# A graph network in four layers: the row fetches of its first two passes are made once a tile, and SyncE copies the rows to their places

## The chip, the cores and the metric

The kernel runs on one core of a Trainium2 chip. The metric is the device time of one execution in microseconds (us), the median of several runs.

## What is computed

The input is a graph of 5000 nodes with 128 features and 85,000 edges sorted by their destination. Four layers each take a layer norm and a ReLU of the node features, gather the rows of the source nodes, combine them over the edges of each destination node, and add the result to the features:

```python
edge_index = jnp.stack([src, dst])
h = jnp.maximum(_layernorm(x, axis=-1), 0.0)
x = x + _L0_gnn_ref(h, src, dst, L0_gnn_W, L0_gnn_b)            # mean of h[src] per dst, then a linear layer
h = jnp.maximum(_layernorm(x, axis=-1), 0.0)
x = x + _L1_gnn_ref(h, src, dst, L1_gnn_W_edge, ...)            # mean of relu(A h[src] + B h[dst]) per dst, then a linear layer
h = jnp.maximum(_layernorm(x, axis=-1), 0.0)
x = x + _L2_gnn_ref(h, edge_index, L2_gnn_W1, ...)              # two graph attention convolutions of 16 heads
h = jnp.maximum(_layernorm(x, axis=-1), 0.0)
x = x + _L3_gnn_ref(h, edge_index, L3_gnn_Wq, ...)              # dot-product attention of 2 heads over the edges
```

## The kernel before

The edges lie in 665 tiles of 128 (`T`), one edge on each partition, and the nodes in 40 blocks of 128 (`NB`). A step is one pair of a tile and a block that has destinations in it. Since the edges are sorted, a tile at the border of two blocks makes two steps, one after the other, and there are 665 + 39 = 704 steps. Eight steps make a group (`G = 8`), so that a pass over the edges has 88 groups (`NG`). Most buffers of a pass are rings of four groups (`RING = 4`).

There are five passes over the edges: `sum_pass` (layer 0), `mlp_pass` (layer 1), and `softmax_pass` three times (twice "gat", once "dot"). Each writes the table of node rows that the next one reads to HBM. In a group of the first two passes the engines do this:

- **POOL** (GpSimd) issues in `fetch_groups` (L1154 to L1169) one indirect DMA for each step, which fetches the rows of the 128 source nodes from the table into `GT`. It first waits for the release of the ring's place, four groups back (`sums` in `sum_pass`, `prodded` in `mlp_pass`), and for the group's indices (`index`).
- **ACT** (ScalarE) copies the eight columns of indices from `srcT` to `srcI` (`copy_index`, L1171 to L1175), four groups ahead; it casts the one-hot matrices `Ob` to f32 (`O`), and in `sum_pass` takes the turned ones out of PSUM (`Ot`, L1287).
- **DVE** (VectorE) builds the one-hot matrices in `sum_pass` (L1307), adds the sums of a group to `acc` (`add_group`, L1242) and counts the edges into `deg` (L1240). In `mlp_pass` it adds the fetched rows to the rows of the destinations (`prod`, L1396).
- **PE** (TensorE) turns the one-hot matrices (L1327) in `sum_pass`, brings node rows to the edges (L1189) in `mlp_pass`, and sums the rows of each step into the places of its nodes (`sum_of_step`, L1230). The last matrix product of L1230 in a group raises `sums`, that of L1327 `turned`, that of L1189 `toedge`.
- **SP** (SyncE) stores the one-hot matrices of `sum_pass` in HBM (L1262 and L1266), and loads them again in the later passes (`load_hots`, L1198 and L1203).

Each engine works through the groups in its own order, and semaphores alone hold the engines together. The order of an engine is written out in a `turn` function for each group, and `sweep` unrolls four groups into the body of a loop. An engine that waits in its `turn` does nothing that stands behind that wait. After the last group of a pass the node blocks are worked on in pairs ("units"): they finish the layer, norm the features, and store the next table.

## Time and profile before

| | us |
|---|---|
| median of 3 runs | 6830.07 |
| the runs | 6825.1 to 6843.93 |
| profiled execution | 6823.64 |
| its span | 6821.9 |
| mean granted clock of PE | 0.636 of full speed |

The profile is of one execution. Busy times are given for each engine (PE matrix products, PEld the loading of their weights, DVE, ACT, POOL, and SP, whose DMA issues stand under SPq). A row of the timeline has the start in us from the beginning of the span, the duration, the engine, the line of the kernel, the operation, and in square brackets how long the engine sat idle before it and what released it. "remote" is a release that the profile cannot put down to an instruction; "issue" is time in which the engine waited for nothing that the profile shows. The spans of POOL are rough.

### The profile page before, as it was taken

What the parts mean: (1) busy time and instruction counts of PE and PEld (TensorE: products, weight loads), DVE (VectorE), ACT (ScalarE), POOL (GpSimd) and SP (SyncE); (2) the same over time, 40 slices, a digit from 0 to 9 for tenths busy, and PEclk for the clock granted to TensorE, in tenths of its full rate; (3) what the DMA queues carried; (4) which work ended last, traced back from release to release, by engine and by line L of the source; (5) the groups of instructions that cost most, each with busy time, mean ns of one, the idle gap of its engine ahead of it and who ended that gap; (6) DMA issues with size and microseconds to landing.
All of it is one profiled execution on the core that took longest, in us unless ns stands there. A gap on an engine that the chain in (4) does not pass through costs nothing.

```text
span 6821.9 us, 113042 instructions
## 1 busy us (share of the span) xinstructions
PE 3345.8 (49%) x30004; PEld 2897.9 (42%) x30005; DVE 2697.0 (40%) x6412; ACT 2103.5 (31%) x6369; POOL 3437.8 (50%) x3641
## 2 busy tenths in 40 slices
PE   1545445444444454454454534444444555555555
PEld 1434334333333343444444534444444455555454
DVE  4222223211111144444444544444445644444445
ACT  1111112222222233444444434444444322222222
POOL 3666664455555525555555355455454444444443
PEclk9565666767776665556555655555666666666666
DMA  4222222222222222222222232222222333333332
GB/s 114 91 87 88 90 85 83 80 74 78 75 76 77 75 56 75 78 78 82 78 78 82 56 83 81 77 78 81 77 77 62 103 97 100 96 98 96 98 95 80
DMA packets 342830, 564.68 MB, mean 83 GB/s; under 512 B 90413, under 2 KB 160957, under 8 KB 342622
## 3 DMA queue, kind: packets, MB, share of 16 engines
q0 software_dynamic: 124288, 289.37, 16.1%
q1 hardware_dynamic: 218354, 273.42, 12.7%
q14 instruction: 145, 1.19, 0.1%
q8 instruction: 43, 0.70, 0.0%
HBM read 490.31 MB, written 72.84 MB: 83 GB/s over the span
## 4 chain that ended last, share of the span: by engine, by line
another core or an unknown queue 48%; DVE 17%; PE 14%; issue 13%; ACT 3%; DVEq 2%; ACTq 1%; POOL 1%; DMA 0%; SPq 0%; POOLq 0%
PE psA L1564 7%; PE psDS L1189 3%; DVE acc L1683 2%; PE psDS L1542 2%; DVE prod L1589 1%; PE psA L1230 1%; DVE lg L1598 1%; DVE seg L1605 1%; DVE lastmax L1615 1%; DVE lastmax L1613 1%; DVE below L1661 1%; DVE V L1670 1%; DVE prod L1396 1%; DVE lastmax L1617 1%
## 5 line engine op out<-in xcount | busy, mean ns | idle before, releaser
L1165 POOL DMA_INDIRECT GT<-table,srcI x3520 | 3355.5, 953 | 3202.6 <-DVE V L1670 1403.7
L1564 PE MATMUL psA<-V,O 128*128 128x144 f32 (+1 forms) x4176 | 988.6, 425 | 10.8 <-ACT psA L1500 5.5
L1189 PE MATMUL psDS<-nodeQ,Ot 128*128 x2816 | 605.7, 390 | 658.3 <-ACT Ot L1181 559.8
L1564 PEld LDWEIGHTS psA<-V,O 128*128 128x128 f32 x4176 | 918.0, 314 | 17.2 <-issue 11.8
L1189 PEld LDWEIGHTS psDS<-nodeQ,Ot 128*128 128x128 f32 x2816 | 544.6, 290 | 696.4 <-issue 691.3
L1519 PE MATMUL psDS<-stageD,Ot 128*128 128x16 bf16 x4224 | 251.4, 173 | 804.2 <-issue 802.9
L1519 PEld LDWEIGHTS psDS<-stageD,Ot 128*128 128x128 bf16 x4224 | 184.3, 102 | 878.2 <-issue 860.4
L1683 DVE TENSOR_TENSOR acc<-acc,psA 128x1296 f32 (+1 forms) x261 | 381.2, 1460 | 413.8 <-remote 349.8
L1661 DVE TENSOR_TENSOR below<-lg,psDS 128x128 f32<-128x128 f32 (+1 forms) x264 | 62.4, 236 | 1157.8 <-remote 1156.6
L1500 ACT COPY psA<-consts 128x1296 f32<-128x1296 f32 (+1 forms) x261 | 315.0, 1207 | 628.4 <-DVE acc L1683 471.9
L1550 PE MATMUL psDS<-newM,Ot 128*128 128x16 bf16 (+1 forms) x6336 | 256.5, 175 | 430.2 <-issue 291.3
L1550 PEld LDWEIGHTS psDS<-newM,Ot 128*128 128x128 bf16 x6336 | 233.7, 102 | 472.2 <-issue 300.4
L1542 PE MATMUL psDS<-lastmax,Ob 128*128 128x17 bf16 (+1 forms) x6336 | 211.5, 173 | 451.6 <-DVE lastmax L1617 391.1
L1396 DVE TENSOR_TENSOR prod<-psDS,GT 128x1024 f32<-128x1024 f32 x88 | 107.6, 1223 | 802.6 <-remote 602.6
L1485 ACT COPY nodeMS<-newM 128x16 f32 x1408 | 307.8, 219 | 337.2 <-ACT nodeMS L1485 242.8
L1542 PEld LDWEIGHTS psDS<-lastmax,Ob 128*128 128x128 bf16 x6336 | 191.3, 103 | 490.5 <-issue 490.5
L1377 ACT ACTIVATE V<-prod 128x1024 f32<-128x1024 f32 x88 | 93.0, 1057 | 842.0 <-DVE prod L1396 680.0
L1670 DVE TENSOR_TENSOR V<-GT,psA 128x1024 f32<-128x1024 f32 x264 | 320.9, 1216 | 67.2 <-ACT psA L1507 66.7
L1224 PE MATMUL psA<-zerob 1*128 1x512 bf16 x352 | 153.2, 528 | 374.6 <-issue 270.9
L1240 DVE TENSOR_TENSOR deg<-deg,psA 128x8 f32 x88 | 14.3, 163 | 812.1 <-remote 787.0
L1230 PE MATMUL psA<-O,GT 128*128 128x128 f32 x1408 | 324.4, 424 | 8.9 <-DMA GT<-table,srcI 8.8
L1507 ACT ACTIVATE psA<-below 128x128 f32<-128x128 f32 (+1 forms) x264 | 65.3, 247 | 851.9 <-DVE below L1664 756.7
(244 smaller groups left out, 5286.0 us busy)
## 6 DMA issues: line engine op xcount, KB each, us to landing
Ob<-onehots SPq DMA_DIRECT2D x352, 256.0 KB
Ot<-onehots_turned SPq DMA_DIRECT2D x352, 256.0 KB
GT<-table,srcI POOLq DMA_INDIRECT x3520
onehots<-Ob SPq DMA_DIRECT2D x88, 256.0 KB
onehots_turned<-Ot SPq DMA_DIRECT2D x88, 256.0 KB
first<-first_dram SPq DMA_DIRECT2D x176, 64.0 KB
first_dram<-GT SPq DMA_DIRECT2D x18, 384.0 KB, 5.1
table<-nodeQ SPq DMA_DIRECT2D x40, 128.0 KB, 1.9
```

The source lines that it names most:

```text
L1165: eng.indirect_dma_start(out=GT[:, p.k, j, 0:table.shape[1]], out_offset=None, in_=table, in_offset=bass.IndirectOffsetOnAxis(ap=srcI[:, p ...
L1189: ins = eng.matmul(psD[:, j, :], Ot32[:, p.q, j, :], at_block(nodeQ, b[j], D), start=True, stop=True)
L1230: return eng.matmul(to, rows, hot, start=False, stop=last, skip_group_check=True)
L1396: eng.tensor_tensor(prod[:, :, :], psD[:, :, :], GT[:, a.k, :, 0:D], ALU.add).then_inc(prodded.sem, 1)
L1485: eng.copy(at_block(nodeM, b[j], h), by_step(newM[:, p.q, 0:HG])[:, :, j]).then_inc(noted.sem, 1)
L1500: eng.copy(last_places if is_last(p) else places, consts[:, 0:1, :].unsqueeze(1).to_broadcast([P, 3, 3, VW]))\
L1519: ins = eng.matmul(dst_logits[:, j, :], Ot[:, p.k, j, :], stageD[:, p.q, j, part * h:(part + 1) * h], start=part == 0, stop=part == 2)
L1542: ins = eng.matmul(maxima[:, j, :], Ob[:, p.k, j, :], part, start=n == 0, stop=n == 2)
L1550: ins = eng.matmul(edge_max[:, j, :], Ot[:, p.k, j, :], part, start=n == 0, stop=n == 2)
L1564: ins = eng.matmul(to, O[:, p.q, j, :], V[:, p.q, j, 0:VW], start=False, stop=j == G - 1, skip_group_check=True)
L1670: eng.tensor_tensor(v[:, :, :, 0:C], heads(GT[:, p.k, :, f0:f0 + D], h), wide(factors, C), ALU.mult)\
L1683: eng.tensor_tensor(to, to, last_places if is_last(p) else places, ALU.add).then_inc(added.sem, 1)
```

## The change

A tile is fetched once in each of the first two passes, 665 indirect DMAs instead of 704, into a second ring of four groups of tiles. These fetches are written out one after another (no loop on POOL), and take their indices from `srcT` in place, so that `srcI` and its copies on ACT are not used there. SyncE waits until the tiles that a group of steps needs have landed, and copies the 128 rows of every step from the ring of tiles to the ring of steps by one plain DMA from SBUF to SBUF, 704 in a pass; where in the ring the tile lies comes from a small table, read into registers. The two rings share the memory of `GT` (`rows_of_edges`). The stage that prepares the tables now also makes the indices in tile order, the three small tables (`slots_of_steps`, `tiles_needed`, `tiles_over`), and puts the indices in step order aside in HBM (`src_steps`) for the three later passes. Those keep `fetch_groups`. Units of the table between the second and third pass use the sums in `acc` instead of free columns of `GT`.

```diff
+        def by_tiles(w):
+            size = RING * G * w
+            return (rows_of_edges[:, 0:size].rearrange("p (r g w) -> p r g w", r=RING, g=G),
+                    rows_of_edges[:, size:2 * size].rearrange("p (n w) -> p n w", w=w))
...
+                eng.dma_start(tile_rows[:, 0:WHOLE, :], src[0:WHOLE * P * P].rearrange("(c p e) -> p c e", p=P, e=P))\
+                   .then_inc(load_sem, 16)
...
+                do(eng.tensor_scalar, rowi[1][:, 0:NT - RING], firsts_of_tiles, -1.0, None, ALU.add)
+                do(eng.tensor_scalar, tiles_over[:, :], rowi[1][:, 0:NT - RING], G.bit_length() - 1, None, ALU.logical_shift_right)
+                do(eng.tensor_tensor, slots_of_steps[:, :], row[2][:, 0:SP_], row[0][:, 0:SP_], ALU.subtract)
...
                 eng.dma_start(blk[:, :], block_dram.rearrange("(a s) -> a s", a=1)).then_inc(block_loaded, 16)
+                eng.wait_ge(prepared, marks["src out"])
+                eng.dma_start(src_steps.rearrange("p (c s) -> p c s", c=SC), tile_rows).then_inc(first_stored, 16)
                 eng.wait_ge(prepared, marks["first"])
...
+        def fetch_tiles(eng, table):
+            tables_stored(eng)
+            to = by_tiles(table.shape[1])[1]
+
+            def has_landed(n):
+                eng.wait_ge(*ring_tiles[n % RING](n // RING, min(G, T - n * G) - 1))
+                eng.sem_inc(landed.sem, 1)
+
+            for n in range(NT):
+                k = n % RING
+                if n >= RING:
+                    eng.wait_ge(*copied(loaded(eng, "over", tiles_over, n - RING, 1, NG - 1, for_waits=True)[0]))
+                    apart(eng)
+                for t in range(n * G, min(n * G + G, T)):
+                    eng.indirect_dma_start(
+                        out=to[:, t % (RING * G), :], out_offset=None, in_=table,
+                        in_offset=bass.IndirectOffsetOnAxis(ap=srcT[:, t:t + 1], axis=0),
+                    ).then_inc(ring_tiles[k].sem, 16)
+                    if t % G == G // 2 and n:
+                        has_landed(n - 1)
...
+        def copy_rows(eng, p, w, release):
+            to, of = by_tiles(w)
+            last = isinstance(p.g, int) and p.g == NG - 1
+            eng.wait_ge(*release(p.g - RING))
+            apart(eng)
+            at = loaded(eng, "slots", slots_of_steps, p.g, G, RING * G - 1)
+            need = loaded(eng, "need", tiles_needed, p.g, 2, NT - 1, for_waits=True)
+            parts = [(0, G // 2, need[0]), (G // 2, G, need[1])]
...
+            for a, z, group in parts:
+                eng.wait_ge(*landed(group))
+                apart(eng)
+                for j in range(a, z):
+                    eng.dma_start(to[:, p.k, j, :], of[:, bass.ds(at[j], 1), :].rearrange("p o w -> p (o w)"))\
+                       .then_inc(ring_rows[p.k].sem, 16)
+
+        def rows_copied(eng, p):
+            eng.wait_ge(*ring_rows[p.k](p.i))
+            eng.sem_inc(copied.sem, 1)
...
 sum_pass:
-                    fetch_groups(eng, NG, table, sums)
+                    fetch_tiles(eng, table)
...
                     def turn(p):
+                        copy_rows(eng, p, D, sums)
+                        rows_copied(eng, p)
                         eng.wait_ge(*onehot(p.g))
...
-                        if p.has(RING):
-                            copy_index(eng, p.plus(RING))
...
 mlp_pass:
-                    fetch_groups(eng, NG, table, prodded)
+                    fetch_tiles(eng, table)
...
-                    sweep(eng, NG, lambda p: load_hots(eng, p, (onehot32,), (turned32,)))
+                    def turn(p):
+                        if p.has(0):
+                            copy_rows(eng, p, D, prodded)
+                        if p.has(1):
+                            load_hots(eng, p.plus(1), (onehot32,), (turned32,))
+                        if p.has(0):
+                            rows_copied(eng, p)
+                    sweep(eng, NG, turn, early=1)
+                    eng.wait_ge(*landed(NT - 1))
+                    eng.dma_start(srcT[:, :], src_steps).then_inc(src_loaded, 16)
```

The order of POOL at the beginning of the sum pass, in the kernel before (names in square brackets are the semaphores that an instruction waits for):

```order
L1165 DMA GT<-table0,srcI 128x128 x7
L1165 DMA GT<-table0,srcI 128x128 [waits sums,index]
L1165 DMA GT<-table0,srcI 128x128 x7
L59 UNCONDITIONAL_BRANCH
L59 ISA
L1162 REGISTER_ALU [waits sums]
```

The same place now; `tiles0` to `tiles3` count the landed fetches of the ring, and `copied` the groups that SyncE has copied:

```order
L1247 DMA rows_of_edges<-table0,srcT 128x128 [waits tiles2]
L1247 DMA rows_of_edges<-table0,srcT 128x128 x2
L200 TENSOR_LOAD tiles_over
L206 ISA
L1247 DMA rows_of_edges<-table0,srcT 128x128 [waits copied]
L1247 DMA rows_of_edges<-table0,srcT 128x128 x4
L1247 DMA rows_of_edges<-table0,srcT 128x128 [waits tiles3]
```

POOL no longer waits for PE's `sums` or ACT's `index`; it waits for SyncE, and, in the middle of each group, for the landing of the group before, which alone tells SyncE that the group is there.

The order of SP in the loop of the sum pass before, one group and the beginning of the next:

```order
L1262 ISA [waits onehot]
L1262 DMA onehots<-Ob 128x1024
L1266 DMA onehots_turned<-Ot 128x1024 [waits onehotT]
L1260 REGISTER_ALU
L1262 ISA [waits onehot]
L1262 DMA onehots<-Ob 128x1024
```

And now, from the last copy of the pass's first group to the first copy of its second (four such pairs of `L1272` follow each wait for `landed`):

```order
L1272 DMA rows_of_edges<-rows_of_edges 128x128
L1379 DMA onehots<-Ob 128x1024 [waits rows0,onehot]
L1383 DMA onehots_turned<-Ot 128x1024 [waits onehotT]
L200 TENSOR_LOAD slots_of_steps [waits sums]
L208 ISA
L200 TENSOR_LOAD tiles_needed
L206 ISA
L1272 ISA [waits landed]
L1272 DMA rows_of_edges<-rows_of_edges 128x128
```

Eight copies, two loads of registers and their landing (`rows0`) stand ahead of the two stores of a group, and the copies of the next group stand behind the wait for `onehotT` of this one.

## Rows read from the trace of the kernel before

**Rows 1.** The page, part 1: busy time of each engine.

```profile
PE 3345.8 (49%) x30004; PEld 2897.9 (42%) x30005; DVE 2697.0 (40%) x6412; ACT 2103.5 (31%) x6369; POOL 3437.8 (50%) x3641
```

**Rows 2.** Stretches: the sum pass, the MLP pass, two stretches of later passes.

```profile
core 0: us, PE busy (x) PEld busy (x) DVE busy (x) ACT busy (x) POOL busy (x), PEclk, DMA share, GB/s
112.00:1142.10 1030.10, 492.27 (x2960) 394.87 (x2960) 225.03 (x265) 180.52 (x256) 662.36 (x696) 0.62 0.29 88
1240.00:2427.30 1187.30, 509.92 (x2845) 434.97 (x2846) 201.37 (x168) 259.28 (x336) 657.23 (x692) 0.69 0.27 75
```

**Rows 3.** Waits of the sum pass, 112 to 1142 us: us, times, longest.

```profile
DVE deg L1240 <- remote: 787.0, 81, 36.2
```

**Rows 4.** Timeline of the sum pass, POOL: ends of its streams of fetches.

```profile
335.10 0.95 POOL L1165 DMA_INDIRECT GT<-table,srcI  x1 [3.95 <-remote]
336.35 0.95 POOL L1165 DMA_INDIRECT GT<-table,srcI  x1 [0.30 <-issue]
...
353.93 0.95 POOL L1165 DMA_INDIRECT GT<-table,srcI  x1 [0.30 <-issue]
358.80 0.95 POOL L1165 DMA_INDIRECT GT<-table,srcI  x1 [3.93 <-remote]
```

**Rows 5.** Timeline of the same stretch, ACT, DVE and PE.

```profile
341.56 1.06 PE L1327 MATMUL psT<-identb,Ob 128*128 128x128 bf16 x8
343.76 0.16 DVE L1240 TENSOR_TENSOR deg<-deg,psA 128x8 f32 x1 [6.88 <-remote]
356.32 1.01 ACT L1287 COPY Ot<-psT 128x1024 bf16<-128x1024 bf16 x1 [11.56 <-remote]
358.08 0.16 DVE L1240 TENSOR_TENSOR deg<-deg,psA 128x8 f32 x1 [11.82 <-remote]
367.42 0.16 DVE L1240 TENSOR_TENSOR deg<-deg,psA 128x8 f32 x1 [6.84 <-remote]
```

**Rows 6.** Timeline of the sum pass's start, behind a stream of 40 fetches.

```profile
112.03 0.95 POOL L1165 DMA_INDIRECT GT<-table,srcI  x1 [52.68 <-ACT srcI L1175]
161.96 0.95 POOL L1165 DMA_INDIRECT GT<-table,srcI  x1 [0.30 <-issue]
168.43 1.04 ACT L1283 CAST O<-Ob 128x1024 f32<-128x1024 bf16 x1 [22.86 <-remote]
```

**Rows 7.** Timeline of the MLP pass, one stream and the next.

```profile
1702.31 0.95 POOL L1165 DMA_INDIRECT GT<-table,srcI  x1 [7.89 <-ACT srcI L1175]
1721.49 0.95 POOL L1165 DMA_INDIRECT GT<-table,srcI  x1 [0.30 <-issue]
1725.04 1.23 DVE L1396 TENSOR_TENSOR prod<-psDS,GT 128x1024 f32<-128x1024 f32 x1 [12.84 <-remote]
1726.18 1.21 DVE L1242 TENSOR_TENSOR acc<-acc,psA 128x1024 f32 x1
1730.12 0.95 POOL L1165 DMA_INDIRECT GT<-table,srcI  x1 [7.67 <-ACT srcI L1175]
1737.33 1.22 DVE L1242 TENSOR_TENSOR acc<-acc,psA 128x1024 f32 x1 [3.85 <-PE psA L1230]
```

**Rows 8.** SP's issues of 64 KB loads; loads of registers; issues of L1203; landing times.

```profile
17.18 0.43 SPq L267 DMA_DIRECT2D V<-in_L_gnn_Wk  x1
17.65 0.43 SPq L267 DMA_DIRECT2D V<-in_L_gnn_Wv  x1
...
L187 PEldq TENSOR_LOAD <-blk_rel x176: 587/592/987, 115.3 to 2502.8; - x176
...
L1203 SPq DMA_DIRECT2D Ot<-onehots_turned x352: 3/332/1677, 1229.7 to 6747.8; - x176
...
table<-V SPq DMA_DIRECT2D x20, 128.0 KB, 1.8
```

**Rows 9.** Timeline of the preparing stage, SP and DVE.

```profile
65.30 22.64 SPq L429 DMA_DIRECT2D first_dram<-GT  x18
65.80 0.96 DVE L336 CAST srcT<-psA 128x768 int32<-128x768 f32 x1 [0.53 <-DVE GT L336]
```

More of the change, by code:

```diff
@@ L50, in has, with sweep @@
         return not isinstance(self.g, int) or 0 <= self.g + d < self.n
-def sweep(eng, n, turn, early=0, late=0):
+def sweep(eng, n, turn, early=0, late=0, tail=0):
     head = -(-late // RING) if late else 1
-    last = (n - early) // RING
+    last = (n - max(early, tail)) // RING
     for p in range(-early, head * RING):
@@ L181, in program, with loaded @@
         reg_sets = {}
-        def loaded(eng, which, table, g, n, most, of=None):
+        def loaded(eng, which, table, g, n, most, of=None, for_waits=False):
             if (eng.engine, which) not in reg_sets:
@@ L187, in loaded @@
             eng.load(regs, table[0:1, bass.ds(g * (of or n), n)])
+            if for_waits:
+                if (eng.engine, which, "held") not in reg_sets:
+                    reg_sets[eng.engine, which, "held"] = [eng.alloc_register(f"{which}_held_{j}") for j in range(n)]
+                held = reg_sets[eng.engine, which, "held"]
+                for r, to in zip(regs, held):
+                    eng.reg_alu(to, r, 0, ALU.max)
+                regs = held
             return [eng.snap(r, min_val=0, max_val=most) for r in regs]
@@ L199, in program @@
         noted.per = G
+        ring_tiles = [Count(sem(f"tiles{r}"), G, 16) for r in range(RING)]
+        landed, copied, src_loaded = Count(sem("landed")), Count(sem("copied")), sem("src_loaded")
         ring_rows = [Count(sem(f"rows{r}"), 1, 16 * G) for r in range(RING)]
@@ L323, in program @@
         TILES, FRESH = 1, 2
-        SRC, SLOTS_, LAST = 1, 2, 3
+        TILE_SRC, SRC, SLOTS_, LAST = 1, 2, 3, 4
         dst_f, src_f, last_r, first_r = rows[2:6]
+        tile_f = rows[7]
+        firsts_of_tiles = work[0:1, 1024:1024 + NT - RING]
+        assert (NT - RING) * G + 1 <= T and 1 << (G.bit_length() - 1) == G and RING * G & (RING * G - 1) == 0
         with nc.Block() as block:
@@ L370, in _ @@
                     do(eng.tensor_copy, WG[k][:, D:D + 2 * HEADS1], psS[:, 64 * k:64 * k + 2 * HEADS1])
+                eng.wait_ge(tables_turned, TILE_SRC)
+                do(eng.tensor_copy, srcT[:, :], psN[:, 0:SC, :].rearrange("p c s -> p (c s)"))
+                marks["tiles out"] = count
                 eng.wait_ge(fetched, 16 * 2 * SC)
@@ L464, in _ @@
                 ins.then_inc(weights_turned, 1)
+                eng.wait_ge(prepared, marks["w1 w2"])
+                turn(tile_f)
+                eng.wait_ge(prepared, marks["tiles out"])
                 eng.wait_ge(prepared, marks["src"])
@@ L1171, in copy_index, with tiles_closed @@
+        def rows_copied(eng, p):
+            eng.wait_ge(*ring_rows[p.k](p.i))
+            eng.sem_inc(copied.sem, 1)
+        def tiles_closed():
+            landed.close(NT)
+            copied.close(NG)
+            for k in range(RING):
+                ring_tiles[k].base += 16 * len([t for t in range(T) if t // G % RING == k])
         def copy_index(eng, p):
             if not (isinstance(p.i, int) and p.i <= 0):
-                eng.wait_ge(*ring_rows[p.k](p.i - 1))
+                eng.wait_ge(*ring_tiles[p.k](p.i - 1))
@@ L1346, in _ @@
                     rest_of_units(eng, phase, phase.tensor)
-            close((index, onehot, turned, onehotT, onehot32, sums, counted, added), NG)
+            close((onehot, turned, onehotT, onehot32, sums, counted, added), NG)
+            tiles_closed()
             rows_closed(NG)
@@ L1370, in turn @@
                             eng.copy(O[:, a.q, :, :], Ob[:, a.k, :, :]).then_inc(onehot32.sem, 1)
-                        if p.has(RING):
-                            copy_index(eng, p.plus(RING))
                         begin_units(eng, phase, phase.scalar, p, 0)
@@ L1419, in _ @@
                     rest_of_units(eng, phase, phase.tensor)
-            close((index, onehot32, turned32, toedge, prodded, values, sums, added), NG)
+            close((onehot32, turned32, toedge, prodded, values, sums, added), NG)
+            tiles_closed()
             rows_closed(NG)
@@ L1817, in _ @@
                     phase.vector(eng)
[L1818 removed]
+            index.close(NG)
+            close((onehot32, toedge, prodded, logit, logitT, segmax, segT, flagged, lastmaxed,
                    lastmax1ed, lastmax2ed, nmax, pens, tmaxed, resets, carried, forward, newMed, newM1ed, newM2ed, drop, rescale,
                    maxedge, belowed, bound, factor, weight, values, emptied, sums, scaled, added, *([staged, noted] if gat else [turned32])), NG)
[L1821 removed]
+            for k in range(RING):
+                for c in (ring_tiles, ring_hot, ring_hotT):
+                    c[k].close(NG // RING)
             phase.over()
```

94 lines of the change are left out of this document (61 added, 33 removed).

## The prediction

> **What bounds the kernel now.** I read the page's busy times first. No engine is busy for more than half of the span [rows 1], so the question is in each pass which wait ends last. The table of stretches gives the two passes that the change touches [rows 2]: the sum pass fetches over 1030 us, the MLP pass over 1187 us and a little more. POOL is the busiest in both, though only for 64% and 55%.
>
> Next come the waits and the timeline of one cycle in the middle of the sum pass. POOL does not fetch evenly: it issues 16 fetches (two groups) in one stream, with 1.25 to 1.26 us from start to start, sits idle for 3.9 us, and begins the next stream 23.70 us after the last one [rows 4]. That is 11.85 us a group, and 88 x 11.85 = 1043 us agrees with the stretch. So POOL's pace is in the cycle, and so is its pause.
>
> What ends the pause stands in the rows of the other engines [rows 5]. PE issues the eight turned matrices of L1327 at 341.56, yet ACT gets to copy them only at 356.32, after 11.56 us of idleness, which is 1.4 us after POOL's last fetch ended (353.93 + 0.95 = 354.88). DVE adds a group at 343.76, the next at 358.08, just before POOL starts again at 358.80, and the third already at 367.42. So in the pause and the first part of a stream a group takes 367.42 - 358.08 = 9.3 us, and in the second part of a stream PE's results come out only when the stream ends. The longest wait of the pass, 787 us of DVE on `sums`, is this one [rows 3]. The start of the pass shows it at its plainest: POOL fetches 40 times without a pause until 162.9, and ACT then waits 22.86 us for PE, until 168.43 [rows 6]. The MLP pass has the same form [rows 7]: stream from 1702.31 to 1722.44, DVE's `prod` at 1725.04 (2.6 us later, 12.84 us idle before it), next stream at 1730.12, 27.81 us for two groups, 13.9 us each. There the pause is 7.67 us, and ends with ACT's copy of the indices. Without a stream's second half a group takes 1737.33 - 1726.18 = 11.15 us.
>
> I take from this that the two passes go in cycles: POOL streams what has been released; PE gets two groups out per stream however long it is, the second when it ends; then a chain of steps lets POOL go on. Why PE's results are held the rows do not say.
>
> **The change part by part.** Each of the two passes loses 39 fetches, 39 x 1.256 = 49 us of POOL. A group then has 665 / 88 = 7.56 fetches, 9.5 us of stream instead of 10.05. This counts in full only if the stream stays the same part of the cycle.
>
> ACT loses 88 index copies of some 0.2 us in each pass. In the sum pass they stand beside waits of ACT for PE, at nothing. In the MLP pass the copy is what ends POOL's pause; what is late next there is the new chain.
>
> The new chain is the price. POOL is now released by SP. In the sum pass, from PE's result on: ACT's copy 1.0 us [rows 5]; SP's store of the turned matrices, about 0.5; two loads of registers, 0.59 each for eight registers, 1.2 together (between 0.6 and 1.2, the second loads two); eight copies at the 0.47 us of a 64 KB load, 3.8; the landing of the last, 1.8, by the median of `table<-V` [rows 8]; POOL's own load of a register, 0.6; its start after a release, 358.80 - 358.08 = 0.7. Sum 9.6 us. With the 1.4 us before it the pause is 11.0 us instead of 3.9. No row shows a copy from SBUF to SBUF. Below, its issue could cost 0.33 us as other SP issues do, and above 1.68, the longest of L1203 [rows 8]; I take 0.47, the row with the same 128 pieces of 512 bytes. SP needs some 1.0 + 1.2 + 3.8 + 1.8 = 7.8 us a group, under the 11.85 of the cycle. The wait for the copies' landing sits ahead of the two stores; ACT waits for the store of four groups earlier, so that delay costs nothing.
>
> The Trainium skill, page "DMA: Bandwidth & Descriptors", section "Anatomy of one DMA — SWDGE (gpsimd) path", gives any DMA on that path a fixed 2.0 us plus bytes over 436 GB/s, mostly completion. For 64 KB that is 2.15 us, where the row has 1.8 us for 128 KB on SP's path. By the page's price each pause would be 0.35 us longer, an estimate of 59 x 0.35 = 20 us more than my sum.
>
> In an 11.0 us pause PE gets one group more out (it needs 9.3), so a cycle covers three groups: stream 3 x 7.56 x 1.256 - 0.3 = 28.2 us, pause 11.0, together 39.2, or 13.07 a group. Against 11.85 that is +1.22 x 88 = +107 us. In the MLP pass the pause is 2.6 + 1.2 (`prod`) + the chain from SP's loads on, 8.1, so 11.9 us; one group (11.15) fits again; (28.2 + 11.9) / 3 = 13.37 against 13.9: -0.53 x 88 = -47 us. There SP's loads for the later step run ahead of PE, so nothing else waits behind the copies.
>
> The preparing stage: SP's stores of `first_dram` end it, 22.64 us from 65.30 on [rows 9]. They now stand behind one more store that waits for DVE's cast ending at 66.76, and takes about 1.3 us itself: +2.8 us. Three more loads at the start: +1.5 to 2.5. DVE's seven one-row operations at the end (about 3 us) lie beside SP's stores. Together +5 us. The reload of `srcT` lies beside the units at the end of the MLP pass, at nothing; if that cover were gone, 2 to 5 us.
>
> Sum: 107 - 47 + 5 = +65 us on the profiled 6823.64, so 6889. The median of the runs lies 6.4 us over that execution: 6895 us.
>
> **The rivals.** First, faster. The two rings give POOL up to eight groups of lead instead of four. If the copies run so far ahead that a pause is as long as before, the cycle keeps two groups and only the stream shrinks: 0.89 fetches x 1.256 = 1.12 us, x 44 x 2 = 98 us, so 6895 - 65 + 5 - 98 = 6737 us. If the lead halves the pauses as well, another 44 x (2.0 + 3.8) = 255 us go, to 6480; the floor with POOL never idle is 835 us a pass. For it: in the MLP pass SP waits only for work three or four groups back. Against it: 40 fetches in a row at the start did not let PE go on [rows 6], and in the sum pass SP's copies stand behind `onehotT`, so their lead is one group, not four. It decides if the pause after the change is under 5 us in both passes.
>
> Second, no change. PE's results may be held for a reason of PE's own and only happen to come with the end of a stream; then its cycle stands whatever POOL does, and 6824 + 5 + 6 = 6835 us. For it: DVE's and ACT's waits are far longer than POOL's. Against it: rows 6. That the fetches do not come down to 665 is part of this case, and unlikely.
>
> Third, much slower, one mechanism: PE does not get its extra group out in the longer pause, because the next fetches or the copies hold its results too. Two groups a cycle then: (18.7 + 11.0) / 2 = 14.9 in the sum pass, +264 us; (18.7 + 11.9) / 2 = 15.3 in the MLP pass, +123 us; with the 5 us, 7222 us. It would be about the same if SP itself became the bound, above 0.9 us a copy (4.0 + 8 x 0.98 = 11.85). It decides when a cycle still has two groups.
>
> **How the numbers follow.** My forecast has a chance of 0.36, the faster rival 0.34, no change 0.15, much slower 0.15. A difference under 0.3% (20 us) can't be told from none here. So faster 0.34, same 0.15, slower 0.51. The forecast's own range is 6850 to 6990. The one that should hold 8 times in 10 goes from 6680, which takes in the faster rival with a part of its further gain, to 7230, which takes in the third.
>
> **What the profile would show.** L1247 with 1330 fetches, and streams of about 23 fetches rather than 16 in the middle of the sum pass, with pauses near 11 us; sum pass about 1150 us of fetching, MLP pass about 1180. SP's copies at 0.4 to 0.5 us from start to start. Wrong if POOL's pauses stay under 5 us or if it streams evenly (faster rival), if the cycle stays at 23.7 us (no change), if the copies take over 0.9 us each or streams keep 15 fetches (third).

## The result, and the profile after

The changed kernel takes 6985.0 us (median of 4 runs, 6974 to 6992), the kernel before 6828.1 us in the same session: ratio 1.0223, 95% interval 1.0203 to 1.0244. It is 157 us slower; 65 us were forecast. The span of the profiled execution is 6983.9 us. The rows of its page that answer to [rows 1] and to the fetches and the copies, first busy times, then groups as "busy, mean ns of one | idle before, releaser":

```profile
PE 3435.5 (49%) x30010; PEld 2989.3 (43%) x30011; DVE 2706.8 (39%) x6422; ACT 2090.5 (30%) x6193; POOL 3366.1 (48%) x3564
L1247 POOL DMA_INDIRECT rows_of_edges<-table,srcT x1330 | 1265.5, 951 | 1258.5 <-SPq L1278 738.8
L1345 PE MATMUL psA<-O,rows_of_edges 128*128 128x128 f32 x1408 | 324.6, 423 | 540.5 <-DMA rows_of_edges<-rows_of_edges 527.9
```

There are 1330 fetches, as the diff says. Most of POOL's idle time before them (739 of 1259 us) is ended by L1278, where SP says that a group's rows are copied. PE waits 528 us for copies. The stretches that answer to [rows 2]:

```profile
core 0: us, PE busy (x) PEld busy (x) DVE busy (x) ACT busy (x) POOL busy (x), PEclk, DMA share, GB/s
115.80:1395.40 1279.60, 486.59 (x2974) 410.16 (x2974) 228.35 (x282) 173.74 (x178) 633.21 (x665) 0.61 0.34 104
1471.00:2585.00 1114.00, 610.85 (x2872) 516.65 (x2872) 209.41 (x169) 259.16 (x256) 632.27 (x665) 0.67 0.41 120
```

The two stretches of [rows 2] leave out fetches of the kernel before: they hold 696 and 692 of 704 (the sum pass goes on to 1152.8, the MLP pass begins at 1230.7 and goes on to 2434.0). From the first fetch to the end of the last they are:

```profile
112.03:1152.90 1040.87, 496.49 (x2974) 397.84 (x2974) 227.19 (x276) 182.25 (x261) 670.59 (x704) 0.62 0.29 88
1230.70:2434.00 1203.30, 518.07 (x2896) 442.45 (x2896) 207.94 (x172) 264.31 (x342) 669.53 (x704) 0.70 0.27 77
```

So the sum pass now fetches for 1279.6 us (its stretch runs 3 us past the last fetch), 14.5 us a group, against 1040.9 and 11.8; the MLP pass for 1114.0, 12.7 a group, against 1203.3 and 13.7. Measured from the pass's first fetch to its last instruction the sum pass is 237 us longer, the MLP pass 85 us shorter, the preparing stage 3.8 us longer and the three later passes together some 6 us longer. The sum is 162 us, and so much do the spans differ. So the loss is all in the sum pass. Its waits, which answer to [rows 3], are us, times, longest:

```profile
PE psA L1345 <- DMA rows_of_edges<-rows_of_edges: 527.9, 81, 13.2
POOL rows_of_edges L1247 <- SPq L1278: 449.6, 71, 23.4
DVE deg L1355 <- issue: 747.2, 63, 13.0
DVE deg L1355 <- remote: 163.6, 8, 31.9
```

PE's products of the rows wait 81 times until the copies have landed. The wait of 787 us [rows 3] has not gone: the part that the profile calls remote is down to 164, but 747 us now stand under "issue", with nothing named. SP itself hardly waits. Its own waits in the pass, all of them:

```profile
SPq L1278 <- DMA rows_of_edges<-rows_of_edges: 97.0, 76, 1.3
SPq L192 <- POOLq L1239: 11.0, 1, 11.0
```

So one turn of SP follows on the other. Most turns look like these two. The first column is the start, the second the time from the first start of the row's instructions to the last one's end:

```profile
409.76 0.34 SPq L1379 DMA_DIRECT2D onehots<-Ob  x1
410.28 0.34 SPq L1383 DMA_DIRECT2D onehots_turned<-Ot  x1
413.14 10.04 SPq L1272 DMA_DIRECT2D rows_of_edges<-rows_of_edges  x8
424.91 0.35 SPq L1379 DMA_DIRECT2D onehots<-Ob  x1
428.33 10.02 SPq L1272 DMA_DIRECT2D rows_of_edges<-rows_of_edges  x8
410.20 0.95 POOL L1247 DMA_INDIRECT rows_of_edges<-table,srcT  x1 [5.42 <-SPq L1278]
425.34 0.95 POOL L1247 DMA_INDIRECT rows_of_edges<-table,srcT  x1 [5.40 <-SPq L1278]
```

SP's turn takes 15.15 us and POOL's cycle 15.14: 8 fetches, then 5.4 us of waiting for SP. The eight copies take 10.0 us. How long they take without a stream beside them shows where POOL falls silent for longer, as it does now and then (nine pauses of 10 to 23 us in the pass). One such place, behind a stream of 15:

```profile
694.30 7.47 SPq L1272 DMA_DIRECT2D rows_of_edges<-rows_of_edges  x8
707.37 0.69 SPq L1379 DMA_DIRECT2D onehots<-Ob  x1
710.87 0.69 SPq L1383 DMA_DIRECT2D onehots_turned<-Ot  x1
716.64 5.25 SPq L1272 DMA_DIRECT2D rows_of_edges<-rows_of_edges  x8
723.61 0.34 SPq L1379 DMA_DIRECT2D onehots<-Ob  x1
724.13 0.34 SPq L1383 DMA_DIRECT2D onehots_turned<-Ot  x1
726.99 3.43 SPq L1272 DMA_DIRECT2D rows_of_edges<-rows_of_edges  x5
```

And POOL's timeline of the same place, the first fetch of the stream of 15, its last, and the next:

```profile
694.15 0.95 POOL L1247 DMA_INDIRECT rows_of_edges<-table,srcT  x1 [1.86 <-issue]
...
711.74 0.95 POOL L1247 DMA_INDIRECT rows_of_edges<-table,srcT  x1 [0.30 <-issue]
734.52 0.95 POOL L1247 DMA_INDIRECT rows_of_edges<-table,srcT  x1 [21.83 <-SPq L1278]
```

One turn of SP goes from 694.30 to 716.64, 22.3 us, and POOL streams through 18.4 of them. The next goes from 716.64 to 726.99, 10.35 us, with POOL silent. It is the same work. In the silent turn the 8 copies take 5.25 us, 1.7 us pass until the first store (the copies' landing), 0.9 until the second is issued, 2.5 until the next copies (two loads of registers and their moves). In the other the same four parts take 7.5, 5.6, 4.2 and 5.1 us. While POOL streams, a store's issue is 0.69 us long instead of 0.34, and two stores that were 0.52 us apart are 3.50 apart. The move of a register ahead of the second store shows the same step (ns min/median/max of the three stores from 690 to 727 us):

```profile
L1383 SPq MOVE onehots_turned<-Ot x3: 29/29/690, 691.4 to 724.1; - x3
```

In the usual turn at 409.76 all parts but the copies have their silent length: the stores (0.9 us) and the loads (2.5) fall into the first 3 us of POOL's stream, the landing (1.7) into its pause. The copies fall into the rest of the stream. PE gets a group's rows only when its copies have landed; from PE's timeline, with its idle time and what ended it:

```profile
702.25 3.78 PE L1345 MATMUL psA<-O,rows_of_edges 128*128 128x128 f32 x16 [3.90 <-DMA rows_of_edges<-rows_of_edges]
```

The MLP pass has another form than the 27.81 us for two groups of [rows 7]. POOL now streams 8 fetches, waits 2.4 to 4.1 us for SP, and streams 8 again:

```profile
1859.83 0.95 POOL L1247 DMA_INDIRECT rows_of_edges<-table,srcT  x1 [3.03 <-SPq L1278]
...
1873.66 0.95 POOL L1247 DMA_INDIRECT rows_of_edges<-table,srcT  x1 [4.08 <-SPq L1278]
...
1885.82 0.95 POOL L1247 DMA_INDIRECT rows_of_edges<-table,srcT  x1 [2.43 <-SPq L1278]
```

From the two traces come a theory A, that SP's turn has become the bound of the sum pass, a theory B, my own from the forecast, that the longer chain from fetch over copy to the next fetch is what costs, and a theory C, that the MLP pass is shorter only because of what the sum pass before it does.

### The profile page after: what moved, and what is told of

Same layout as the page of the kernel before. It is cut to its first block, busy times and chain, and to the rows that moved or that the text cites. A ratio compares the mean times of both kernels' runs of the same rounds, so it can differ in the third digit from the quotient of the medians.

```text
span 6983.9 us, 117608 instructions
## 1 busy us (share of the span) xinstructions
PE 3435.5 (49%) x30010; PEld 2989.3 (43%) x30011; DVE 2706.8 (39%) x6422; ACT 2090.5 (30%) x6193; POOL 3366.1 (48%) x3564
## 3 DMA queue, kind: packets, MB, share of 16 engines
q0 software_dynamic: 121792, 284.25, 14.5%
## 4 chain that ended last, share of the span: by engine, by line
another core or an unknown queue 24%; issue 22%; SPq 20%; DVE 15%; PE 11%; DMA 3%; ACT 1%; DVEq 1%; POOL 1%; ACTq 0%; POOLq 0%
SPq L1272 11%; PE psA L1688 8%; SPq L200 3%; DMA rows_of_edges<-rows_of_edges 2%; DVE acc L1807 2%; SPq L192 2%; PE psDS L1666 2%; DVE rows_of_edges L1713 1%; DVE lg L1722 1%; DVE seg L1729 1%; DVE lastmax L1739 1%; DVE lastmax L1737 1%; DVE below L1785 1%; SPq L1313 1%
## 5 line engine op out<-in xcount | busy, mean ns | idle before, releaser
L1225 POOL DMA_INDIRECT rows_of_edges<-table,srcI x2112 | 2018.2, 956 | 2176.7 <-DVE V L1794 1409.8
L1247 POOL DMA_INDIRECT rows_of_edges<-table,srcT x1330 | 1265.5, 951 | 1258.5 <-SPq L1278 738.8
L1304 PE MATMUL psDS<-nodeQ,Ot 128*128 x2816 | 657.6, 415 | 485.1 <-ACT Ot L1296 264.2
L1304 PEld LDWEIGHTS psDS<-nodeQ,Ot 128*128 128x128 f32 x2816 | 589.3, 312 | 525.3 <-issue 519.9
L1345 PE MATMUL psA<-O,rows_of_edges 128*128 128x128 f32 x1408 | 324.6, 423 | 540.5 <-DMA rows_of_edges<-rows_of_edges 527.9
L1345 PEld LDWEIGHTS psA<-O,rows_of_edges 128*128 128x128 f32 x1408 | 301.1, 325 | 547.3 <-issue 547.2
L1398 ACT CAST O<-Ob 128x1024 f32<-128x1024 bf16 x88 | 92.0, 1045 | 1074.7 <-issue 774.5
L1519 DVE TENSOR_TENSOR rows_of_edges<-psDS,rows_of_edges 128x1024 f32<-128x1024 f32 x88 | 107.7, 1223 | 697.5 <-remote 315.6
```

Of the source, the lines that this page charges most:

```text
L1225: eng.indirect_dma_start(out=GT[:, p.k, j, 0:table.shape[1]], out_offset=None, in_=table, in_offset=bass.IndirectOffsetOnAxis(ap=srcI[:, p ...
L1247: eng.indirect_dma_start(out=to[:, t % (RING * G), :], out_offset=None, in_=table, in_offset=bass.IndirectOffsetOnAxis(ap=srcT[:, t:t + 1] ...
L1304: ins = eng.matmul(psD[:, j, :], Ot32[:, p.q, j, :], at_block(nodeQ, b[j], D), start=True, stop=True)
L1345: return eng.matmul(to, rows, hot, start=False, stop=last, skip_group_check=True)
```

## The experiments

Each time is a median, with the ratio to the kernel before on the same chip and its 95% interval.

**e1, the new scheme in the MLP pass alone.** In the sum pass:

```diff
-                    fetch_tiles(eng, table)
+                    fetch_groups(eng, NG, table, sums)
...
-                        copy_rows(eng, p, D, sums)
-                        rows_copied(eng, p)
...
+                        if p.has(RING):
+                            copy_index(eng, p.plus(RING))
```

and in its SP block, at the end, `eng.dma_start(srcT[:, :], src_tiles)`, which the MLP pass's POOL waits for.

> The sum pass is as in the kernel before, the MLP pass as in the changed one (the table of row numbers in order of steps stands in SBUF during the sum pass, the one in order of tiles is loaded from DRAM between the passes). Theory A (in the sum pass SP's turn, with its loads, 8 copies and 2 stores, is the bound; in the MLP pass SP has room): the MLP pass keeps its -85 us, the sum pass goes back to 1117 us, so 6828 - 85 + 4 (preparation) + 3 (the load between) = 6750 us. Theory B (the loss is POOL's longer pause, from streamed fetches to copies) says the same here. Theory C (the MLP pass is shorter only because the sum pass before it was longer and rested the clock or moved work of the units): the MLP pass takes 1302 us again, 6835 us.

Measured: 6768.9 us, 0.9912 (0.9895 to 0.9928). This half alone is faster than both kernels. C is out as the whole cause: the MLP pass fetches for 1129.0 us, some 74 less than before. That is 15 us more than in the changed kernel, and what makes these 15 us is not known.

**e2, the new scheme in the sum pass alone** (the same edit, made in the MLP pass).

> The other half alone: the sum pass of the changed kernel, the MLP pass of the one before. Theories A and B: +237 in the sum pass, +4 of preparation, nothing in the MLP pass: 7070 to 7080 us. Theory C: the MLP pass takes 1217 us although it is the old one, 6990 us.

Measured: 7062.6 us, 1.0340 (1.0322 to 1.0357). -60 and +233 make 173, so the two halves add up to the change's 157 within 16 us: nearly independent, not wholly.

**e3, half of the copies.** `some` is true in the sum pass alone:

```diff
-                for j in range(a, z):
+                for j in (range(a, z) if not some else range(a, min(z, a + (3 if last and not a else 2)))):
```

> In the sum pass SP copies 4 of a group's 8 rows (the other 4 rows stay zero, so 4 of 8 steps' sums are left out; PE does all its products). Theory A: 4 copies of 0.65 us in quiet time and up to twice 0.7 us while POOL streams leave SP's turn, 2.6 to 5.6 us of 14.5 us a group, down to what the rest of the pass takes, 11.7 us a group: 2.6 to 2.8 us x 88 = -230 us, 6755 us (6740 to 6800). Theory B: the copies stand once a cycle of three groups between POOL's stream and its next one: 4 x 0.65 x 29 = -76 us, 6910 us.

Measured: 6884.2 us, 1.0085 (1.0064 to 1.0106): 101 us less than the changed kernel. A's 230 is wrong, B's 76 is nearer. The trace says why. POOL, idle time before its fetch in brackets, and DVE:

```profile
708.36 0.95 POOL L1248 DMA_INDIRECT rows_of_edges<-table,srcT  x1 [6.51 <-SPq L1279]
737.79 0.95 POOL L1248 DMA_INDIRECT rows_of_edges<-table,srcT  x1 [9.63 <-SPq L1279]
```

```profile
712.99 0.17 DVE L1356 TENSOR_TENSOR deg<-deg,psA 128x8 f32 x1 [5.53 <-PE psA L1346]
731.68 0.17 DVE L1356 TENSOR_TENSOR deg<-deg,psA 128x8 f32 x1 [16.20 <-remote]
739.22 0.17 DVE L1356 TENSOR_TENSOR deg<-deg,psA 128x8 f32 x1 [5.04 <-PE psA L1346]
```

POOL streams 16 fetches again, and from stream to stream are 29.4 us, in which DVE adds two groups. That is the cycle of [rows 4, 5] with pauses of 6.5 to 9.6 us instead of 3.9. Over the pass POOL waits for SP 40 times, 8.5 us on average, where it waited 71 times. So SP's turn is the first bound of the changed kernel, and the cycle with a longer pause the second, 1.2 us a group below it (1175.9 us of fetching, 13.4 a group).

**e4, ACT issues the two stores.** In the sum pass SP's two `dma_start` of L1379 and L1383 stand behind ACT's copy of `Ot` instead.

> In the sum pass ACT issues the two stores of the one-hot matrices, right behind its own copies; SP only loads registers and copies rows. Theory A: SP's turn loses two stores and two waits, about 1.5 us in quiet time and 5 us while POOL streams, and stands no longer behind onehotT: 14.5 us a group becomes 12 to 12.5, -180 to -220 us, 6785 us (6760 to 6850); ACT, 34% busy, takes the two issues. Theory B: SP's stores stand outside the chain from copies to fetches, no more than 1 us of each cycle: -30 us to nothing, 6955 to 6985 us.

Measured: 6904.5 us, 1.0112 (1.0093 to 1.0132), 80 us less than the changed kernel, where A gave 200 and B 30 at most. The sum pass fetches for 1187.3 us, 13.5 a group, and POOL waits for SP 37 times, 8.6 us on average. That is e3's form, by another way: both end at the second bound.

**e5, the changed kernel with half of the fetches in the sum pass.** `each` is `G // 2` there and `G` in the MLP pass:

```diff
-                for t in range(n * G, min(n * G + G, T)):
+                for t in range(n * G, min(n * G + each, T)):
```

> The changed kernel with 4 of 8 tiles fetched in each group of the sum pass (the others stay zero, so half of the sums are left out; all copies and products are done). Theory A2 (SP's turn is the bound: 10.4 us where POOL is quiet, 14.5 on average because SP's instructions take 0.7 us each while POOL streams): POOL streams 5 us of each group instead of 10, the turn becomes about 12.4 us, 2.1 x 88 = -185 us, 6800 us. Theory B2 (the stretch of SP's instructions has nothing to do with POOL, and POOL's stream is hidden since POOL waits anyway): no change, 6960 to 6985 us.

Measured: 6644.6 us, 0.9724 (0.9708 to 0.9740): 340 us less than the changed kernel, nearly twice what A2 gave. SP's timeline:

```profile
512.71 5.85 SPq L1273 DMA_DIRECT2D rows_of_edges<-rows_of_edges  x8
520.26 0.34 SPq L1380 DMA_DIRECT2D onehots<-Ob  x1
524.15 5.45 SPq L1273 DMA_DIRECT2D rows_of_edges<-rows_of_edges  x8
```

With streams of 4 fetches SP's instructions nearly keep their length, and the pass takes 930.1 us of fetching, 10.6 us a group, against 10.35 for SP's turn in the silent stretch. POOL waits for SP 79 times. So it is SP's turn that bounds the pass, and POOL's stream that lengthens the turn. B2 is out.

**e6, the kernel before with half of the fetches in the sum pass** (`for j in range(each)` in `fetch_groups`, with `each` as `G // 2` in this pass).

> The kernel before with 4 of 8 rows fetched in each group of the sum pass (the others stay zero, so half of the sums are left out). Theory P (what PE, ACT and DVE hand on is held up by POOL's stream): with a stream of half the length a group takes 8 to 9 us instead of 11.8, -240 to -330 us, 6500 to 6590 us. Rival (PE's results come two groups at a time for a reason of its own, as in the second rival of the prediction): the cycle stays at 23.7 us, 6830 us.

Measured: 6409.2 us, 0.9380 (0.9364 to 0.9396), 423 us less. The 352 fetches left out are 442 us of POOL, in a pass in which POOL was busy for 64% [rows 2]; nearly all of them come off the time. A stretch and two waits of the run:

```profile
114.70:739.80 625.10, 455.28 (x2964) 385.20 (x2964) 226.82 (x275) 177.44 (x259) 335.45 (x352) 0.69 0.34 109
```

```profile
DVE deg L1241 <- PE psA L1231: 376.6, 80, 5.1
POOL GT L1166 <- PE psA L1231: 197.7, 80, 2.9
```

A group takes 7.1 us, and DVE's wait for PE is 5.1 us at most and has PE named, where it was up to 36.2 us and "remote" [rows 3]. The rival of e6 is out, and the gain is larger than theory P gave (240 to 330 us): POOL's stream keeps PE's results back, and with half of it they come at once.

**e7, copies that nobody waits for**, in the kernel before's sum pass, ahead of SP's stores:

```diff
...
+                        for j in range(8):
+                            eng.dma_start(GT[:, p.k, j, D:2 * D], ident[:, :]).then_inc(ring_idle[p.k].sem, 16)
```

> The kernel before, with 8 copies of 64 KB from SBUF to SBUF (a constant, into halves of the ring that this pass doesn't use) issued by SP ahead of each group's two stores in the sum pass; nothing waits for them but SP's own next round of the ring. Theory A2: SP's turn becomes 17 or so instructions; at 0.7 us each while POOL streams that is about 12 us, a little over the 11.8 us of a group: 0 to +60 us, 6830 to 6890 us. Theory of contention (the copies' traffic slows fetches and stores): 8 x 64 KB more a group make the sum pass as long as in the changed kernel, +150 to +240 us. Theory that only the chain from fetch over copy to fetch counts: 0.

Measured: 6880.9 us, 1.0078 (1.0061 to 1.0095), +49 us, inside what A2 gave. The copies' traffic alone is not the +237.

**e8, the stores ahead of the wait for the copies.** In the changed kernel's sum pass:

```diff
-                        copy_rows(eng, p, D, sums)
-                        rows_copied(eng, p)
...
+                        if p.has(0):
+                            copy_rows(eng, p, D, sums)
+                        b = p.plus(-1)
...
+                        if p.has(0):
+                            rows_copied(eng, p)
```

> The changed kernel, with SP in the sum pass issuing a group's copies, then the two stores of the group before it, and only then waiting for the copies to land and telling POOL. Theory A2 (SP's turn is the bound): the 1.8 us of landing are filled with the stores' instructions, up to -1.8 x 88 = -130 us, I take 6900 us. Theory B (the chain from copies to POOL's next stream is the bound): POOL is told 1 to 5 us later a group, +30 to +150 us, 7015 us or more.

Measured: 6873.2 us, 1.0065 (1.0048 to 1.0082), 112 us less than the changed kernel. POOL is told later and the pass is shorter, 1167.0 us of fetching, 13.3 a group, near the 13.4 and 13.5 of e3 and e4. `b` is the group whose two stores are issued there. Theory B as the first bound is out.

**e9, e10, e11** then fell on a chip of another kind. e9 has the sum pass of before and reads the rows in place in the MLP pass:

```diff
-                            eng.tensor_tensor(prod[:, :, :], psD[:, :, :], by_tiles(D)[0][:, a.k, :, :], ALU.add).then_inc(prodded.sem, 1)
...
+                                for j in range(x, z):
+                                    ins = eng.tensor_tensor(
+                                        prod[:, j, :], psD[:, j, :],
+                                        by_tiles(D)[1][:, bass.ds(at[j], 1), :].rearrange("p o w -> p (o w)"), ALU.add)
```

> As e1 (sum pass of before, MLP pass with each tile fetched once), but without copies: DVE adds each step's row to its product straight from the slot that the fetch wrote, 8 additions of 128 x 128 in place of one of 128 x 1024, waits for the fetches itself, and the addition frees the slot. SP only loads the one-hot matrices. Theory A3 (in the MLP pass too SP's turn, stretched by POOL's stream, is the bound of the e1 form): POOL waits no more for SP; the pass goes towards POOL's own 665 x 1.256 = 835 us plus its pauses, 1231 becomes 1100 to 1180 us, so 6770 - 90 = 6680 us (6640 to 6720). Rival (DVE's own instructions with addresses in registers take 0.7 us each while POOL streams, 8 of them 5.6 us a group, or PE, DVE and ACT are the bound): 6770 to 6850 us.

e10 is e3's edit in the MLP pass:

> The changed kernel with 4 of 8 rows copied in each group of the MLP pass (the others are what the ring held before, so the sums of those steps are wrong; all other work is done). Theory A3 (the MLP pass is bound by SP's turn too: 13 us a group, all of it instructions and POOL waits for its last one): 4 copies less are 2.6 us less, down to what the others need: -100 to -200 us, 6830 us. Rival (the MLP pass is bound by PE's results held while POOL streams, and SP's turn only ends near POOL's wait): -30 us to nothing, 6955 to 6985 us.

and e11 is the kernel before with `table.rearrange("n (a e) -> (n a) e", e=w)` as the source of the sum pass's fetches, `w` being half a row:

> The kernel before, the sum pass fetching pieces of 256 bytes in place of rows of 512 (the same number of fetches with the same indices, half the bytes, other data, so its sums are wrong). Theory P1 (what holds the others is that POOL issues fetches, 128 row descriptors each, whatever their bytes): no change, 6825 to 6840 us. Theory P2 (it is the fetches' traffic): with half the bytes more than half of the 423 us that half the fetches gave, 6600 us or less.

Measured: 4888.2, 4944.6 and 4915.3 us, with 4913.2 us for the kernel before: 0.9952 (0.9935 to 0.9968), 1.0068 (1.0051 to 1.0085), 1.0006 (0.9996 to 1.0016). The kernel before takes 28% less time there with the same program. The expectations were for the first kind of chip and can't be judged by these.

**e12 to e15** ran on a second chip of that kind.

> The kernel of e9 again, since e9 to e11 ran on a chip on which the kernel before takes 4913 us and SP's instructions show no steps of 0.7 us. Where the kernel before takes 6830 us: theory A3 6680 us (6640 to 6720), since no copies and no wait for SP are left; rival (DVE's 8 additions with registers take 0.7 us each while POOL streams) 6770 us or more. Where it takes 4913 us: 4888 us again.

> The kernel of e11 again (sum pass of before fetches 256 bytes a row; its sums are wrong). Where the kernel before takes 6830 us: theory P1 (the number of fetches and their descriptors holds the others up) 6825 to 6840 us; P2 (their bytes) 6600 us or less. Where it takes 4913 us: 4915 us again.

> The kernel of e10 again (the changed kernel, 4 of 8 rows copied in the MLP pass, sums of the others wrong). Where the kernel before takes 6830 us: theory A3 (SP's turn is the bound of the MLP pass too) 6830 us; rival 6955 to 6985 us. Where it takes 4913 us: 4945 us again.

> The changed kernel itself on this chip. Where the kernel before takes 6830 us it takes 6985 us. Where that takes 4913 us, SP's turn in the sum pass is 10.4 us, under what a group takes (883 us of fetching for 88 groups, 10.0 us), or just at it: theory A (what is lost is lost to the stretch of SP's instructions) says within 1% of before, 4900 to 4960 us; the rival that the chain from fetch to copy to fetch costs +157 us by itself says 5070 us.

Measured: 4888.8, 4916.1, 4947.4 and 4947.0 us with 4911.5 before: 0.9952 (0.9936 to 0.9969), 1.0009 (0.9999 to 1.0018), 1.0074 (1.0057 to 1.0091), and for the changed kernel 1.0073 (1.0056 to 1.0089). So the change loses 36 us there, not 157: the rival of e15, 5070 us, is out. The other times are within 3 us of what was expected for this kind of chip. Half of the copies (e14) save nothing in the MLP pass on this kind of chip. SP in the changed kernel on this chip:

```profile
600.13 5.29 SPq L1272 DMA_DIRECT2D rows_of_edges<-rows_of_edges  x8
607.72 0.34 SPq L1379 DMA_DIRECT2D onehots<-Ob  x1
611.13 3.94 SPq L1272 DMA_DIRECT2D rows_of_edges<-rows_of_edges  x6
```

POOL streams beside this turn but for 1.4 us, and nothing is stretched. The moves of registers ahead of the copies show it over both passes (ns min/median/max), and the second stores give SP's mean turn from their first and last start (87 turns), first on the chip of the result, then on this one:

```profile
L1272 SPq FUSED_REGOPS  x1408: 2/55/1624, 127.2 to 2609.7; - x176
L1383 SPq DMA_DIRECT2D onehots_turned<-Ot x88: 3/338/708, 136.5 to 1423.0; - x88
```

```profile
L1272 SPq FUSED_REGOPS  x1408: 55/55/95, 127.5 to 1960.8; - x176
L1383 SPq DMA_DIRECT2D onehots_turned<-Ot x88: 332/338/357, 135.5 to 1063.1; - x88
```

The mean turn is 14.8 us on the one and 10.7 on the other, with the same instructions.

The two passes of the changed kernel on this chip, and of e13 (the same fetches as before in number and order, in the MLP pass also in bytes):

```profile
115.70:1036.90 921.20, 485.55 (x2994) 412.25 (x2995) 230.28 (x291) 172.00 (x183) 633.26 (x665) 0.64 0.50 144
1113.10:1951.50 838.40, 552.61 (x2915) 464.13 (x2916) 214.37 (x202) 264.52 (x268) 632.42 (x665) 0.75 0.57 161
```

```profile
115.90:1000.50 884.60, 503.13 (x3104) 425.07 (x3104) 243.46 (x346) 196.41 (x297) 670.25 (x704) 0.64 0.28 78
1047.90:1931.60 883.70, 600.32 (x2954) 506.83 (x2955) 216.95 (x210) 268.00 (x361) 669.40 (x704) 0.71 0.37 105
```

Here POOL's stream never stops in e13: 884.6 / 704 = 1.256 us a fetch, 10.05 us a group. With the change the MLP pass's fetching follows POOL down, -45 us for 39 fetches. The sum pass can't: SP's turn of 10.7 us is 0.6 us more than POOL's 8 fetches, and its stretch of fetches is 37 us longer. The rest of the loss stands behind the last fetches: from the first fetch of a pass to that of the next, the sum pass is 65 us longer than in e13 (997.4 against 932.0) and the MLP pass 35 us shorter (928.5 against 963.3). That makes 31 us, and the spans differ by 32.

**e16 and e17**, the kernels of e1 and e9 side by side, on a chip of the first kind:

> The kernel of e1 again. Where the kernel before takes 6830 us: 6770 us again. Where it takes 4912 us: the changed kernel's MLP pass took 928 us there against 961 us of before, so 4912 - 33 + 4 + 3 = 4886 us; if SP's copies cost that chip something even here, 4912 us or more.

> The kernel of e9 beside e16 on one chip. Where the kernel before takes 6830 us: theory A3 (SP's stretched turn is the bound of the MLP pass of e1) 6680 us (6640 to 6720); rival (DVE's 8 additions with registers are stretched instead, or PE is the bound) 6770 us or more. Where it takes 4912 us: 4888 us again.

Measured: 6858.4 and 6875.6 us with 6896.1 before: 0.9943 (0.9926 to 0.9960) and 0.9967 (0.9955 to 0.9980). The gain of e1 is 38 us here, where it was 60. Without any work of SP between fetch and addition the MLP pass is no shorter (1164.8 us of fetching against 1146.7). Waits of e17's MLP pass:

```profile
DVE rows_of_edges L1531 <- issue: 425.0, 87, 28.1
POOL rows_of_edges L1249 <- DVE rows_of_edges L1531: 333.1, 50, 21.0
```

POOL now waits for DVE as long as it waited for SP in e16 (322 us). Theory A3, 6680 us, is out: taking SP's turn away does not shorten the MLP pass. But DVE's addition has also become eight with moves of registers between them, 0.28 us each for one of 1.22, so these runs do not say what bounds the pass in e1.

**e18**, e11 once more:

> The kernel of e11 again (sum pass of before fetches 256 bytes a row; its sums are wrong). Where the kernel before takes 6830 to 6900 us: theory P1 (the number of fetches and their descriptors holds the others up) within 0.3% of before; P2 (their bytes) -200 us or more, 6600 to 6700 us. Where it takes 4912 us: 4915 us again.

Measured: 4923.9 us with 4918.9 before, 1.0010 (1.0000 to 1.0019), again on the second kind of chip. Whether it is the number of fetches or their bytes that stretches the others stays open.

## Why the prediction was right and wrong

The sign held, and 6985 us lies in the forecast's own range, but the size did not hold (+65 forecast, +157 measured), and the two terms behind it came about in other ways than I had them.

**The reading of the cycle was right, and its cause is now shown.** That PE's results come out when POOL's stream ends [rows 5, 6] was read from rows only. e6 shows it: half of the fetches take 423 us from a pass in which POOL was busy for 64%. So the second rival, no change, rested on something that is not so.

**The step that failed is SP's turn**: "7.8 us a group, under the 11.85 of the cycle". The same four parts read 10.35 us in a silent stretch. The copies are 5.25 us and not 3.8: 0.65 us from start to start, with a move of a register (0.06) ahead of each issue and 0.51 for the issue itself, where 0.47 was taken from loads with fixed addresses, whose issue is 0.43. The two loads of registers with their moves are 2.5 and not 1.2. Landing (1.7) and stores (0.9) were right; the estimate of 20 us more, with a landing of 2.15 us, did not come true. And that is the smaller half. While POOL streams, SP's own instructions are stretched: the copies take 10.0 us in the usual turn, which is then 15.15 us long, 14.8 on average, and the pass's fetching comes to 14.5 us a group. My sum has SP at 7.8 us and no term for this. The page of before held the warning: issues of L1203 went from 3 over 332 to 1677 ns [rows 8]; I used the 1677 as an upper bound for one copy instead of asking when SP's instructions take that long. The stretch is in register moves too (0.69 us for one of 0.03, up to 1624 ns), which move no data, so a share of the DMA engines doesn't explain it. The Trainium skill, page "DMA: Bandwidth & Descriptors", section "SWDGE vs HWDGE vs iDMA", says that POOL's and SP's transfers stand in different queues of each engine, which serves them in turn. That rule is of transfers, and the trace shows more than it covers: the DMA share is 0.34 in this pass, and a register move takes 0.69 us. What in POOL's stream holds the other engines' instructions is not shown. My condition for the third rival was right (SP as the bound above 11.85 us a turn, above 0.9 us a copy; a copy takes 1.25 us in the usual turn), and its chance of 0.15 was too low. That its price of 14.9 us a group is near the 14.5 measured is luck: it was worked out from two groups a cycle with a pause of 11.0 us, and its +123 us in the MLP pass did not come.

**Three groups in a cycle** (13.07 us a group, +107 us) failed too, and is hidden behind the first. e3 and e4, where SP has room, go mostly in cycles of two groups, 29.4 us in the one shown of e3, 13.4 to 13.5 us a group over the pass. A group more in the longer pause did not fit. With this alone the pass would have been some +135 us (1175.9 - 1040.9), an estimate, since e3 makes half of the copies.

**The MLP pass**: -47 forecast, -85 measured, of fetching -89 and in e1 -74. The sign was for the wrong reason. The pauses in the stretch shown are 2.4 to 4.1 us (4.1 on average over 71 waits), not 11.9, since POOL is released group by group, and the streams are 8 fetches and not 23. In short streams less is held back. That it is the shorter streams that gain is an argument from e5 and e6, which show it for the sum pass; in the MLP pass itself it was not tried. Reading in place instead of copying gains nothing: 0.9967 against 0.9943, with intervals that overlap.

**The rest.** 39 fetches are worth about the 49 us taken only where POOL never pauses: 45 us of fetching in the MLP pass of the second kind of chip, of which 35 are left at the end of the pass. The preparing stage was 3.8 us longer, 5 forecast. Streams of 23 fetches with pauses of 11 us, the sign that I named, are nowhere in the middle of the sum pass: the streams there are of 8 fetches, but for five of 15. Of the two signs of the third rival the copies of over 0.9 us are there, the steady streams of 15 are not.

A version that beats both kernels is e1, with the new scheme in the MLP pass alone: 0.9912 and 0.9943 in two sessions on the first kind of chip. It was not run on the second kind, where its relative e9 has 0.9952.

## What to carry to other kernels

Price a helper queue by the whole turn it makes for each group (moves and loads of registers, waits, landing), and set that against the pace of the pass, not only its place in the chain. Price it at the length that its instructions have while the neighbour that it serves is at work: a spread such as 3/332/1677 ns in one line asks for the place where the long ones stand. And where a change splits by stage into a gain and a loss, run the halves: here one is 60 us faster than before, and together they are 157 us slower.

## What the runs showed of the hardware

- The same program takes 6828 to 6896 us on some chips and 4912 to 4919 us on others, at a granted clock of 0.64 and 0.69 of full speed (mean of the span). A fetch costs POOL 1.26 us on both (15 starts in 18.83 us before [rows 4]; 884.6 us for 704 in e13). On the first kind SP's instructions come to some 0.7 us each in the later part of a stream of fetches (0.69 for a move of 0.03 and for a store's issue of 0.34), and behind a long stream PE's results reach ACT and DVE when it ends [rows 5, 6]; on the second neither is seen (e15: moves 55 to 95 ns; e13: DVE waits for PE 8.0 us at most, beside a stream that never stops). The first softmax pass, which the change leaves alone, takes 1399 us on the one and 975 on the other (its first fetch to the first of the next pass, kernel before and e11). What differs between the chips no trace says.
- With streams of 4 fetches in place of 8 or 15 the stretch is nearly gone (e5: eight copies in 5.5 to 5.9 us, against 10.0 in the usual turn and 5.25 in silence), on the first kind of chip.
- A copy of 64 KB from SBUF to SBUF with a source address in a register costs SP 0.65 us where nothing stretches it, with 1.7 us from the last one's issue to the store behind the wait for its landing.
